# Where two groups of values and one projection of keys stand among the jobs of a graph attention kernel

## The chip, the cores and the metric

The kernel runs on one core of one Trainium2 chip. The metric is the device time in microseconds (us) of one execution. The input is fixed: 32 graphs of 256 nodes with 384 features, in float32.

## The reference, cut to what matters

For every graph, 12 heads of 32 features attend over 256 nodes, restricted to the edges of an adjacency matrix. The input is added back, and each row is normalised:

```python
q = split(x @ Wq + bq);  k = split(x @ Wk + bk);  v = split(x @ Wv + bv)   # 32 x 12 x 256 x 32
scores = q @ k.T / sqrt(32) + beta * adj
scores = where(adj > 0, scores, -9e15)
out = softmax(scores) @ v                       # per head, 256 x 32
x = layernorm(x + merge(out))                   # 32 x 256 x 384
```

## The kernel before, in words

All five engines run one long unrolled program, and semaphores join them. The 12 heads of a graph form three groups of four. TensorE computes the scores of a group at once (`scores`, line 463): 16 matmuls, each on a quarter of the array's rows (the profile writes 32*128), into four PSUM banks `s_bank`, one for each head of the group. VectorE then takes the maxima of a head from its bank (line 600), and ScalarE the exponentials (line 518). The exponentials of ten heads of a graph are turned by VectorE in blocks of 32 (line 635) and moved by DMAs into `shuffled`; those of heads 10 and 11 are turned by TensorE.

Everything else that TensorE does is a job, named by a letter, a part and a graph:

- X: a third of the input of a graph is transposed (line 396, two matmuls). ScalarE copies the high half out of PSUM (line 538) and VectorE then subtracts it to get the low half (line 616).
- K, Q: one group of keys or queries (line 387, nine matmuls of 256 columns), copied out by ScalarE (line 534).
- V: half of the nodes' values (line 384, nine matmuls of 384 columns), copied out by ScalarE (line 536).
- T: the exponentials of one head are turned (line 433, four matmuls), copied out by ScalarE (line 530).
- O: probabilities times values for one group of heads (`values`, line 416, 16 matmuls, each on a quarter of the array's columns, written 128*32), copied out by ScalarE (line 544).
- G: the result of an O job is turned back (`turn_heads`, line 424, two matmuls) and scaled by VectorE (line 623).

While the kernel works at the softmax of graph n, its jobs make the input of graph n + 2, the queries, keys and values of graph n + 1, and the output of graph n - 2. The function `jobs_of(n, h)` says by hand which jobs stand at head h. TensorE runs the jobs of head 0, then the second group's scores; those of heads 1 to 4, then the third group's scores; those of heads 5 to 8, then the first scores of graph n + 1; and then those of heads 9 to 11.

All jobs share four PSUM banks, `j_bank`, in rotation. The list `ring` is every job in program order, and the job at place r writes bank r modulo 4. Before its first instruction TensorE waits in `run` until the job at place r - 4 has been copied out, by ScalarE and VectorE both (`wait_taken`). ScalarE does the exponentials of head h + 2 and then takes the jobs of head h. VectorE has its own fixed order around head 9: the maxima of the next graph's head 0, the low half of the X job of head 9, the maxima of the next graph's head 1.

Of the kernel before, what the change touches and what calls it, by code (L numbers as in the profile page):

```python
# [34 lines left out]
def graph_attention_program(nc, x, adj, wq, bq, wk, bk, wv, bv, beta, out):  # L35
# [22 lines left out]
    def by_blocks(n, h):  # L58
        return h < block_heads(n)
# [5 lines left out]
    def jobs_of(n, h):  # L65
        if n == 0:

            jobs = {
                0: (("K", 2, 0),),
                1: (("K", 0, 1),),  # L70
                2: (("Q", 0, 1),),
                3: (("K", 1, 1),),
                4: (("V", 0, 0),),
                5: (("Q", 1, 1),),
                6: (("V", 1, 0), ("Q", 2, 1)),
                7: (("V", 0, 1),),
                9: (("X", 0, 2), ("K", 2, 1)),
                10: (("X", 1, 2),),
                11: (("X", 2, 2), ("V", 1, 1)),
            }  # L80
        elif n < B - 1:
            jobs = {
                0: (("O", 0, n - 2),),
                1: (("X", 0, n + 2), ("K", 0, n + 1)),
                2: (("G", 0, n - 2), ("Q", 0, n + 1)),
                3: (("K", 1, n + 1),),
                4: (("O", 1, n - 2),),
                5: (("X", 1, n + 2), ("Q", 1, n + 1)),
                6: (("G", 1, n - 2), ("Q", 2, n + 1)),
                7: (("V", 0, n + 1),),  # L90
                8: (("O", 2, n - 2),),
                9: (("X", 2, n + 2), ("K", 2, n + 1)),
                10: (("G", 2, n - 2),),
                11: (("V", 1, n + 1),),
            }
        else:
            jobs = {
                0: (("O", 0, n - 2),),
                1: (("O", 1, n - 2),),
                2: (("G", 0, n - 2), ("O", 2, n - 2)),  # L100
                3: (("G", 1, n - 2),),
                4: (("G", 2, n - 2),),
                5: (("O", 0, n),),
                7: (("G", 0, n), ("O", 0, n - 1)),
                8: (("O", 1, n - 1),),
                9: (("G", 0, n - 1), ("O", 2, n - 1), ("G", 1, n - 1), ("O", 1, n)),
                10: (("G", 2, n - 1), ("G", 1, n)),
            }
        turn = () if by_blocks(n, h) else (("T", h, n),)
        return turn + tuple(job for job in jobs.get(h, ()) if 0 <= job[2] < B)  # L110
# [4 lines left out]
    second_jobs = (("K", 1, 0),) + tuple(("X", c, 1) for c in range(C))  # L115
    last_jobs = (("O", 2, B - 1), ("G", 2, B - 1))
    ring = [*first_jobs, *second_jobs, *(job for n in range(B) for h in range(H) for job in jobs_of(n, h)), *last_jobs]
    place = {job: r for r, job in enumerate(ring)}

# [33 lines left out]
    with ctx:  # L153
# [216 lines left out]
        def _(pe):  # L370
# [124 lines left out]
            for n in range(B):  # L495
                for h in range(H):
                    jobs = jobs_of(n, h)
                    if not by_blocks(n, h):
                        run(jobs[0])
                        jobs = jobs[1:]  # L500
                    for job in jobs:
                        run(job)
                    if h % J == 0:
                        if h < H - J:
                            scores(n, h // J + 1)
                        elif n + 1 < B:
                            scores(n + 1, 0)
# [4 lines left out]
        def _(act):  # L512
# [58 lines left out]
            for n in range(B):  # L571
                for h in range(H):
                    s = H * n + h
                    if s + 2 < B * H:
                        exps(s + 2)
                    for job in jobs_of(n, h):
                        take(job)
# [388 lines left out]
```

## Time and profile before

| quantity | us |
|---|---|
| median of three runs | 622.64 (622.37 to 623.55) |
| the profiled execution's own time | 621.97 |
| its span | 620.1 |
| TensorE (PE) busy | 601.8, 97% |
| VectorE (DVE) busy | 582.7, 94% |
| ScalarE (ACT) busy | 574.8, 93% |
| GpSimd (POOL) busy | 492.6, 79% |

The profile comes from one execution. "PE" are TensorE's matmuls, "PEld" its weight loads, which run beside them. The ends of matmuls are modelled and the next one starts before the end of the last, so that for TensorE the starts are what can be compared. The granted clock of TensorE is shown as 1.00 (of 2.4 GHz) from 60 to 550 us.

### The profile page before, as it was taken

The page shows a single profiled execution, that of the slowest core. Times are in us where ns is not written, and L with a number is a line of the kernel's source. Part 1 is how long each engine was busy: PE and PEld are TensorE (multiplying, and loading weights), DVE is VectorE, ACT ScalarE, POOL GpSimd, SP SyncE. Part 2 cuts the span into 40 slices and gives each one's busy share as a digit, 9 for nine tenths or more (in the row PEclk, how much of TensorE's full clock was granted, in tenths as well). Part 3 has the DMA queues.
Part 4 walks back from the last instruction along what each step waited for, and adds up shares of the span by engine and source line. Part 5 has one row for each costly group of instructions (what it writes and reads, how often), then busy time and mean ns, then how long its engine had stood idle before and what let it go on. Part 6 is the DMA issues. An engine that isn't in the chain of part 4 may idle for free. (4 is left out here: it accounts for less than half of the span.)

```text
span 620.1 us, 20691 instructions
## 1 busy us (share of the span) xinstructions
PE 601.8 (97%) x6080; PEld 488.2 (79%) x6080; DVE 582.7 (94%) x2235; ACT 574.8 (93%) x2063; POOL 492.6 (79%) x669
## 2 busy tenths in 40 slices
PE   8999999999999999999999999999999999999991
PEld 7887878787888878787878788888878787878760
DVE  4989999999999999999999999999999999999786
ACT  4999999999999999999999999999999999999981
POOL 1334448988888888888898888898888889889793
PEclk9999999999999999999999999999999999999996
DMA  6258879988888988888998888898888898887832
GB/s 202 80 120 193 180 169 220 203 193 203 200 201 198 236 177 202 201 203 195 220 199 196 203 201 199 202 222 185 203 202 200 197 227 187 201 201 176 198 92 101
DMA packets 56190, 117.61 MB, mean 190 GB/s; under 512 B 10512, under 2 KB 12304, under 8 KB 56080
## 3 DMA queue, kind: packets, MB, share of 16 engines
q1 hardware_dynamic: 54992, 116.10, 80.6%
q8 instruction: 50, 0.82, 0.6%
q14 instruction: 60, 0.49, 0.3%
q10 hardware_dynamic: 1088, 0.20, 0.2%
HBM read 22.94 MB, written 12.58 MB: 57 GB/s over the span
## 5 line engine op out<-in xcount | busy, mean ns | idle before, releaser
L518 ACT ACTIVATE probs<-neg_scores,neg_max 128x256 f32<-128x256 f32 x768 | 382.5, 504 | 1.8 <-DVE neg_max L600 1.3
L600 DVE CUSTOM_DVE_ANT_0 neg_scores<-s_bank,bias_sb 128x256 f32<-128x256 f32 x768 | 280.1, 414 | 16.3 <-PE s_bank L463 15.1
L635 DVE STREAM_TRANSPOSE blocks<-probs 128x512 f32<-128x512 f32 x308 | 196.8, 685 | 0.3 <-ACT probs L518 0.3
L518 ACT ACTIVATION_READ_ACCUMULATOR probs<-neg_scores,neg_max 128x1 f32 x768 | 150.9, 197 | 0.0
L463 PE MATMUL s_bank<-qk 32*128 32x256 f32 x1536 | 110.0, 400 | 1.0 <-ACT qk L534 0.6
L387 PE MATMUL j_bank<-xt_high,w_high 128*128 128x256 f32 x567 | 110.1, 302 | 0.3 <-ACT qk L534 0.3
L534 ACT ACTIVATE qk<-j_bank,qk_bias 128x256 f32<-128x256 f32 x192 | 89.9, 469 | 21.0 <-PE j_bank L387 17.6
L463 PEld LDWEIGHTS s_bank<-qk 32*128 32x128 f32 x1536 | 69.5, 184 | 41.0 <-ACT qk L534 13.1
L898 POOL TENSOR_SCALAR att<-att,rstd,shift 128x384 f32<-128x384 f32 x58 | 95.7, 1656 | 6.3 <-POOL shift L895 6.3
L416 PE MATMUL j_bank<-shuffled,v_sb 128*32 128x256 f32 x1232 | 98.1, 385 | 0.2 <-ACT blocks L530 0.2
L387 PE MATMUL j_bank<-xt_high,w_low 128*128 128x256 f32 x567 | 97.0, 279 | 0.0
L387 PE MATMUL j_bank<-xt_low,w_high 128*128 128x256 f32 x567 | 96.9, 279 | 0.0
L862 POOL TENSOR_TENSOR att<-att,x_sb 128x768 f32<-128x768 f32 x30 | 55.5, 1850 | 39.2 <-DVE att L623 38.4
L387 PEld LDWEIGHTS j_bank<-xt_high,w_high 128*128 128x128 f32 x567 | 79.4, 189 | 2.3 <-issue 1.8
L387 PEld LDWEIGHTS j_bank<-xt_low,w_high 128*128 128x128 f32 x567 | 79.7, 188 | 0.0
L387 PEld LDWEIGHTS j_bank<-xt_high,w_low 128*128 128x128 f32 x567 | 79.6, 188 | 0.0
L843 POOL TENSOR_SCALAR bias_sb<-adj_sb 128x512 f32<-128x512 f32 x30 | 59.9, 1998 | 22.4 <-DMA adj_sb<-in_adj_dram 16.7
L846 POOL TENSOR_SCALAR adj_sb<-adj_sb,beta_col 128x512 f32<-128x512 f32 x31 | 62.1, 2004 | 13.3 <-DVE bias_sb L648 10.2
L856 POOL TENSOR_TENSOR x_sb<-x_sb,bv_row 128x768 f32<-128x768 f32 x32 | 59.1, 1848 | 8.2 <-DMA bv_row<-in_L_gnn_bv_dram 7.9
L416 PEld LDWEIGHTS j_bank<-shuffled,v_sb 128*32 128x32 f32 x1232 | 37.2, 109 | 35.2 <-issue 15.1
L600 DVE DVE_READ_ACCUMULATOR2_ANT neg_max<- 128x1 f32 x768 | 63.9, 83 | 0.0
L888 POOL TENSOR_SCALAR nt_b<-var_eps,rstd 128x1 f32<-128x1 f32 x174 | 58.3, 347 | 6.5 <-POOL rstd L881 6.2
(81 smaller groups left out, 918.4 us busy)
## 6 DMA issues: line engine op xcount, KB each, us to landing
shuffled<-blocks SPq DMA_DIRECT2D x480, 160.0 KB, 4.2
x_sb<-in_x_dram SPq DMA_DIRECT2D x32, 384.0 KB, 6.1
out_dram<-att SPq DMA_DIRECT2D x30, 384.0 KB, 4.0
adj_sb<-in_adj_dram SPq DMA_DIRECT2D x32, 256.0 KB, 6.2
shuffled<-blocks SPq DMA_DIRECT2D x16, 128.0 KB, 2.5
blocks<-in_L_gnn_Wq_dram SPq DMA_DIRECT2D x1, 576.0 KB, 5.7
blocks<-in_L_gnn_Wk_dram SPq DMA_DIRECT2D x1, 576.0 KB, 8.0
blocks<-in_L_gnn_Wv_dram SPq DMA_DIRECT2D x1, 576.0 KB, 5.0
```

What stands on the lines that cost most here:

```text
L387: mm = pe.matmul(b[:, 0:N], wp[:, q, c, a * P:(a + 1) * P], xp[:, n % 2, c, :], start=(m == 0), stop=(m == 3 * C - 1))
L416: mm = pe.matmul(b[HD * j:HD * (j + 1), 0:N], v_sb[:, n % 4, k, h * HD:(h + 1) * HD], probs_k, start=(k == 0), stop=(k == T - 1))
L463: mm = pe.matmul(s_bank[j][:, t * N:(t + 1) * N], qk[rows, n % 2, 0, g, t * P:(t + 1) * P], qk[rows, n % 2, 1, g, :], start=True, stop=True)
L518: nc.scalar.activation(probs[:, (T * s + t) % (T * NX), :], neg_scores[:, (T * s + t) % (T * NH), :], ACT.Exp, bias=neg_max[:, n % 2, t, h ...
L534: ins = nc.scalar.activation(qk[:, n % 2, q, a, :], b[:, 0:N], ACT.Identity, bias=qk_bias[:, q, a:a + 1])
L600: nc.vector.tensor_tensor_reduce(neg_scores[:, (T * s + t) % (T * NH), :], s_bank[h % J][:, t * N:(t + 1) * N], bias_sb[:, n % 2, t, :], - ...
L635: nc.vector.transpose(blocks[:, n % 2, :, h, :, :].rearrange("p k t q -> p t k q"), probs[:, slot:slot + T, :].rearrange("p t (k q) -> p t ...
L843: nc.gpsimd.tensor_scalar(key_order(bias_sb[:, n % 2, :, :]), by_keys(adj_sb[:, :, :]), 0.0, MASKED, ALU.is_le, ALU.mult).then_inc(not_edg ...
L846: nc.gpsimd.tensor_scalar(adj_sb[:, :, :], adj_sb[:, :, :], 0.0, beta_col[:, 0:1], ALU.max, ALU.mult).then_inc(adj_beta_ready, 1)
L856: nc.gpsimd.tensor_tensor(x_sb[:, n % XB, :, :], x_sb[:, n % XB, :, :], bv_row[:, :].unsqueeze(1).to_broadcast([P, T, D]), ALU.add).then_i ...
L888: b_at[t] = link(nc.gpsimd.tensor_scalar(nt_b[:, t:t + 1], var_eps[:, t:t + 1], rstd[:, t:t + 1], rstd[:, t:t + 1], ALU.mult, ALU.mult))
L898: nc.gpsimd.tensor_scalar(att[:, n % 3, t, :], att[:, n % 3, t, :], rstd[:, t:t + 1], shift[:, t:t + 1], ALU.mult, ALU.subtract).then_inc( ...
```

## The change

Only the table in `jobs_of` for the graphs in the middle (1 to 30) changes. The O job of the second group moves from head 4 to head 0, directly behind the O job of the first group. The K job of the third group moves from head 9 to head 4, where the O job stood.

```diff
         elif n < B - 1:
             jobs = {
-                0: (("O", 0, n - 2),),
+                0: (("O", 0, n - 2), ("O", 1, n - 2)),
                 1: (("X", 0, n + 2), ("K", 0, n + 1)),
...
-                4: (("O", 1, n - 2),),
+                4: (("K", 2, n + 1),),
...
-                9: (("X", 2, n + 2), ("K", 2, n + 1)),
+                9: (("X", 2, n + 2),),
```

No instruction is added or taken away. Since the bank of a job follows from its place in the ring, the banks turn with it. These are TensorE's rows of before from the X job of head 9 to the second scores (their first row only) in the middle of the program; the number behind `j_bank` is the bank:

```order
L396 MATMUL j_bank1<-ident,x_sb 128x128 x2
L387 MATMUL j_bank2<-xt_high,w_high 128x256 x3
L387 MATMUL j_bank2<-xt_low,w_high 128x256 x3
L387 MATMUL j_bank2<-xt_high,w_low 128x256 x3
L433 MATMUL j_bank3<-ident,probs 128x128 x4
L424 MATMUL j_bank0<-ident,heads_t 128x128 x2
L433 MATMUL j_bank1<-ident,probs 128x128 x4
L384 MATMUL j_bank2<-w_high,xt_high 128x384 x3
L384 MATMUL j_bank2<-w_high,xt_low 128x384 x3
L384 MATMUL j_bank2<-w_low,xt_high 128x384 x3
L416 MATMUL j_bank3<-shuffled,v_sb 32x256 x8
L463 MATMUL s_bank0<-qk 128x256
```

And the same place in the changed kernel:

```order
L396 MATMUL j_bank2<-ident,x_sb 128x128 x2
L433 MATMUL j_bank3<-ident,probs 128x128 x4
L424 MATMUL j_bank0<-ident,heads_t 128x128 x2
L433 MATMUL j_bank1<-ident,probs 128x128 x4
L384 MATMUL j_bank2<-w_high,xt_high 128x384 x3
L384 MATMUL j_bank2<-w_high,xt_low 128x384 x3
L384 MATMUL j_bank2<-w_low,xt_high 128x384 x3
L416 MATMUL j_bank3<-shuffled,v_sb 32x256 x8
L416 MATMUL j_bank0<-shuffled,v_sb 32x256 x8
L463 MATMUL s_bank0<-qk 128x256
```

The K job has gone from behind the X job, and the second O job has come. V (line 384) wrote the bank that K had used, and now writes the bank that X has used (2 in both rows); the second T (line 433) wrote X's bank before.

The other place on TensorE is ahead of the third scores, before:

```order
L387 MATMUL j_bank0<-xt_high,w_high 128x256 x3
L387 MATMUL j_bank0<-xt_low,w_high 128x256 x3
L387 MATMUL j_bank0<-xt_high,w_low 128x256 x3
L416 MATMUL j_bank1<-shuffled,v_sb 32x256 x8
L463 MATMUL s_bank0<-qk 128x256
```

and now:

```order
L387 MATMUL j_bank1<-xt_high,w_high 128x256 x3
L387 MATMUL j_bank1<-xt_low,w_high 128x256 x3
L387 MATMUL j_bank1<-xt_high,w_low 128x256 x3
L387 MATMUL j_bank2<-xt_high,w_high 128x256 x3
L387 MATMUL j_bank2<-xt_low,w_high 128x256 x3
L387 MATMUL j_bank2<-xt_high,w_low 128x256 x3
L463 MATMUL s_bank0<-qk 128x256
```

The O job between the second group's keys and the third scores has become the third group's keys.

## Rows read from the trace of the kernel before

**Rows 1.** Window: stretch, length, busy time (and count) by engine, clock, DMA.

```profile
311.47:329.82 18.35, 18.35 (x193) 14.91 (x189) 17.87 (x70) 17.64 (x65) 16.32 (x23) 1.00 0.88 203
```

**Rows 2.** Waits from 60 to 550 us: waiter, releaser, total, times, longest (us).

```profile
DVE neg_scores L600 <- PE s_bank L463: 10.2, 27, 1.0
```

**Rows 3.** Timeline, PE, first scores to second: start, duration, instruction.

```profile
305.30 1.15 PE L463 MATMUL s_bank<-qk 32*128 32x256 f32 x16
306.37 0.44 PE L396 MATMUL j_bank<-ident,x_sb 128*128 128x128 f32 x2
...
307.72 0.60 PE L433 MATMUL j_bank<-ident,probs 128*128 128x128 f32 x4
308.15 0.38 PE L424 MATMUL j_bank<-ident,heads_t 128*128 128x128 f32 x2
308.37 0.60 PE L433 MATMUL j_bank<-ident,probs 128*128 128x128 f32 x4
308.73 0.77 PE L384 MATMUL j_bank<-w_high,xt_high 128*128 128x384 f32 x3
...
310.47 1.07 PE L416 MATMUL j_bank<-shuffled,v_sb 128*32 128x256 f32 x16
...
311.47 1.15 PE L463 MATMUL s_bank<-qk 32*128 32x256 f32 x16
```

**Rows 4.** Timeline, PE, second group's keys, second O job, third scores.

```profile
315.17 0.52 PE L387 MATMUL j_bank<-xt_high,w_high 128*128 128x256 f32 x3
...
315.88 0.52 PE L387 MATMUL j_bank<-xt_high,w_low 128*128 128x256 f32 x3
316.32 1.07 PE L416 MATMUL j_bank<-shuffled,v_sb 128*32 128x256 f32 x16
317.32 1.15 PE L463 MATMUL s_bank<-qk 32*128 32x256 f32 x16
```

**Rows 5.** Timeline, PE, second and fourth round of an O job.

```profile
322.88 0.39 PE L416 MATMUL j_bank<-shuffled,v_sb 128*32 128x256 f32 x2
...
323.31 0.39 PE L416 MATMUL j_bank<-shuffled,v_sb 128*32 128x256 f32 x2
```

**Rows 6.** Timeline, graphs 0 and 1: scores straight behind a K job, a maximum.

```profile
18.24 0.51 PE L387 MATMUL j_bank<-xt_high,w_low 128*128 128x256 f32 x3
18.68 1.15 PE L463 MATMUL s_bank<-qk 32*128 32x256 f32 x16
...
42.08 0.51 PE L387 MATMUL j_bank<-xt_high,w_low 128*128 128x256 f32 x3
...
42.47 0.08 DVE L600 DVE_READ_ACCUMULATOR2_ANT neg_max<- 128x1 f32 x1
...
42.70 1.15 PE L463 MATMUL s_bank<-qk 32*128 32x256 f32 x16
```

**Rows 7.** Timeline, DVE: maxima, low half of X, G job; last, maxima behind third scores.

```profile
306.64 0.42 DVE L600 CUSTOM_DVE_ANT_0 neg_scores<-s_bank,bias_sb 128x256 f32<-128x256 f32 x1 [0.37 <-PE s_bank L463]
...
307.43 0.42 DVE L616 TENSOR_TENSOR xt_low<-j_bank,xt_high 128x256 fp32r<-128x256 f32 x1
...
308.57 0.42 DVE L623 TENSOR_TENSOR att<-j_bank,inv_sum 128x256 f32<-128x256 f32 x1
...
318.74 0.38 DVE L600 CUSTOM_DVE_ANT_0 neg_scores<-s_bank,bias_sb 128x256 f32<-128x256 f32 x1
```

**Rows 8.** Timeline, ACT: end of head 11's exponentials, then the high half of X.

```profile
306.93 0.19 ACT L518 ACTIVATION_READ_ACCUMULATOR probs<-neg_scores,neg_max 128x1 f32 x1
...
307.02 0.37 ACT L538 ACTIVATE xt_high<-j_bank 128x256 fp32r<-128x256 f32 x1
```

**Rows 9.** Timeline in graph 0: a T job held by the low half of X.

```profile
34.29 0.42 DVE L616 TENSOR_TENSOR xt_low<-j_bank,xt_high 128x256 fp32r<-128x256 f32 x1 [0.74 <-ACT xt_high L538]
...
34.78 0.42 PEld L433 LDWEIGHTS j_bank<-ident,probs 128*128 128x128 f32 x4 [0.36 <-ACT qk L534]
```

## The prediction

> **What bounds the kernel now.** I read the page's shares first: PE 97%, DVE 94%, ACT 93% leave no engine much room. I then took one graph in the middle as a window [rows 1]. It lasts 18.35 us, and the matmul row is busy for all of it; VectorE works 17.87 us, ScalarE 17.64. The table of waits shows VectorE waiting for scores once per graph: 10.2 us in 27 times is 0.38 each [rows 2]. It is the wait for the first scores of the next graph [rows 7], and on no other scores does VectorE wait, so TensorE's order sets the period, and VectorE could follow a graph down to about 18.35 - 0.38 = 17.97. What counts is when TensorE starts each job.
>
> I count from the start of the first scores, 305.30 [rows 3]. X starts at 1.07, T at 2.42 (K lies between), V at 3.43, O at 5.17, the second scores at 6.17. From there to the third scores it is 317.32 - 311.47 = 5.85 [rows 3, 4]. The rest of a graph, 6.33 from third scores to first, is untouched.
>
> **Stretch 1, first scores to second: K leaves, O comes.** Without a wait, TensorE would go X, T, G, T, V. A pair of transposes ahead of a T takes 0.22 (308.15 to 308.37), T to G 0.43 (307.72 to 308.15), the second T to V 0.36 [rows 3]. V could start at 1.07 + 0.22 + 0.43 + 0.22 + 0.36 = 2.30, that is 1.13 earlier than now.
>
> But V's bank is now X's. Of X's copies the late one is the low half on VectorE: it starts at 307.43 and takes 0.42, so it ends at 307.85, which is 2.55 [rows 7]. It can't come earlier. On VectorE it stands behind the two maxima of head 0, which wait for the first scores [rows 7]; these are pinned to our zero. On ScalarE the high half it needs runs from 307.02 to 307.39 [rows 8], behind work fed by the part of the graph that doesn't change. Before, the job that used X's bank was the second T, at 3.07: it had half a microsecond to spare. In graph 0 a T job was held by just such a low half: that ended at 34.29 + 0.42 = 34.71 and the weights of T began to load at 34.78, 0.07 later [rows 9]. (The releaser printed there is another, since the wait is for two engines; the low half ended last.) So V starts at 2.55 + 0.07 = 2.62 and not at 2.30: the wait costs 0.32 us in each graph. Nothing covers it: TensorE works in order, and O and the second scores are queued behind.
>
> The other new neighbours don't bind. The first T wants the bank of the third group's queries, copied long before. The second T needs the exponentials of head 11, which end at 306.93 + 0.19 = 307.12, at 1.82 [rows 8]; it wants to start at 1.94, and even 0.1 late it is hidden by V's wait. The second O wants G's bank, which VectorE frees at 308.57 + 0.42, at 3.69 [rows 7]; O comes after 4.
>
> V to O stays 310.47 - 308.73 = 1.74. O behind O is not in the trace. An O job is four rounds; two last 323.31 - 322.88 = 0.43 [rows 5], so four back to back give 0.86, the lower end. The upper end is O as it stands now, with the change of array shape on both sides: 1.00 to the scores [rows 4] and 0.08 ahead of it (K's last triple to O takes 0.44, K's own step is (315.88 - 315.17)/2 = 0.36), 1.08. I take 0.90: the shape stays, which puts it near the lower end, with a little for the new weights. Then the last O to the second scores, 1.00. Sum: 2.62 + 1.74 + 0.90 + 1.00 = 6.26 against 6.17: **+0.09**.
>
> **Stretch 2, second scores to third: O leaves, K comes.** From the start of the second group's keys to the third scores it is now 317.32 - 315.17 = 2.15 [rows 4]. After: one K job at 3 x 0.355 = 1.06, the new one's first to last triple 0.71, and last triple to scores. That last step is in the trace twice: 0.44 in graph 0 (18.24 to 18.68) and 0.62 in graph 1 (42.08 to 42.70) [rows 6]. In the second, the last of the maxima that those scores must wait for ended only at 42.47 + 0.08 = 42.55 [rows 6], so that one holds a wait and I take 0.44; the lower end is K's own 0.36, the upper 0.62. Sum 2.21: **+0.06**. The new K's bank (the first group's keys) and the banks of those after it are freed as before or earlier.
>
> ScalarE gets an O copy (0.37) ahead of head 3's exponentials and loses a K copy (0.47) behind X; its sum stays, and it has 0.71 us idle per graph [rows 1]. VectorE's list doesn't change. The maxima that each set of scores must wait for are earlier relative to it, since both stretches grow. The third scores come 0.15 later after the first ones; VectorE now takes them at 318.74, 1.42 after their start, where it can at 1.34 [rows 4, 7], so it may wait 0.07 there, out of its 0.38. DMA and GpSimd work is the same and follows.
>
> **Sum.** +0.15 us per graph. V's wait exists where a graph has both an X job at head 9 and a G job of an earlier graph: graphs 2 to 29, 28 times. 28 x 0.15 = 4.2 us. In graphs 1 and 30 K moves without the wait, worth under 0.1 each way; I leave them at nothing. The profiled execution took 621.97 (span 620.1 and 1.9 around it) and would take 626.2. The median shown is 0.67 above it, so I predict 622.64 + 4.2 = **626.8 us**, slower by 0.7%.
>
> A rule weighed: the Trainium skill says (TensorEngine Tiling (Array Packing), Key Properties) that changing the tiling mode drains TensorE. The change has one such switch fewer per graph, eight against nine. The trace agrees that a switch costs something: 0.44 against 0.36 from K into O, and 1.00 against 0.86 from O's first round to the scores [rows 4, 5]. By the rule alone the kernel gets faster; the size is the first rival's, which stands on rows.
>
> **Rivals.**
> 1. *No wait for V's bank, only the saved switches: faster.* V at 2.30 gives stretch 1 = 5.94, -0.23; with stretch 2, -0.17 per graph, -4.8 us: 617.9. VectorE's floor of 17.97 per graph would let it through. For it: each of the steps is a row. Against: the low half's end at 2.55 is fixed by two engines. It decides if the low half ends before 2.25. Chance 0.18, with what lies between it and no change.
> 2. *It comes out even.* The wait is there, but O behind O costs 0.86 and K into scores 0.36: +0.15 - 0.04 - 0.08 = +0.03 per graph, 0.8 us, 623.5. Chance 0.10.
> 3. *Switches are not saved at all.* O behind O 1.08, K into scores 0.62: 0.15 + 0.18 + 0.18 = +0.51, 14.3 us, 636.9. Against: the 0.62 holds a wait. Chance 0.07, mostly for a part of it.
> 4. *ScalarE falls behind:* its second O copy pushes X's high half, and with it VectorE's low half and the maxima of heads 6 and 7, by up to 0.37. VectorE's 0.38 of idle time takes that up; only beyond it does it show. With both fully on the path +0.37 x 28 = 10 us more, 637. Chance 0.03.
>
> **Numbers.** Forecast 0.62, its own range 624.0 to 630.5 (O behind O at 0.86 to 1.00, K into scores 0.36 to 0.50, the wait 0.05 either way). A difference of 0.2%, 1.25 us, is about what a measurement of this kernel can tell from none. Slower 0.62 + 0.07 + 0.03 = 0.72, same 0.10, faster 0.18. For 8 in 10 the range is 618.5 to 630.5: below it some 0.08, above it 0.1.
>
> **What would show it.** In a graph of the changed profile: the weight load of V (line 384) behind the second T idle for about 0.3 us, released by VectorE's low half (line 616) or put down to ScalarE; V's first matmul 2.6 us after the first scores; O to O about 0.9; K's last triple to the third scores 0.44; the period 18.50. The first rival is right if V starts at 2.3 and the period is 18.2. The third shows as O to O above 1.0. VectorE's wait at the first scores should stay at 0.4 to 0.5, with a second small one at the third scores. Were the granted clock to leave 1.00 in the middle, all of it would be off.

## The result: slower by 0.9%

| quantity | before | after |
|---|---|---|
| median of four runs, us | 622.50 (622.25 to 623.55) | 627.78 (626.88 to 629.17) |
| ratio of the runs, 95% interval | 1 | 1.0089 (1.0076 to 1.0101) |
| span of the profiled execution, us | 620.1 | 627.3 |

The forecast was 626.8 (range 618.5 to 630.5), 4.2 us above before; measured are 5.3 at the medians. In a second measurement of the same kernel, five rounds on one chip with the experiments below, it took 627.44 against 622.81, ratio 1.0072 (1.0058 to 1.0086).

The profile of the changed kernel, its first part (busy time, share of the span, instructions):

```profile
span 627.3 us, 20691 instructions
PE 606.3 (97%) x6080; PEld 493.1 (79%) x6080; DVE 585.6 (93%) x2235; ACT 575.2 (92%) x2063; POOL 491.3 (78%) x669
```

The counts are those of before; every engine does the same work, TensorE in more time. The span grew by 7.2 us, more than the medians, and part of that isn't the change. Windows of the changed kernel's profile show it: two graphs, and the start (columns: stretch, length, busy time and count of PE, PEld, DVE, ACT, POOL, granted clock, DMA share, GB/s):

```profile
317.34:335.89 18.55, 18.51 (x192) 15.09 (x188) 18.01 (x70) 17.64 (x66) 16.26 (x23) 1.00 0.87 201
335.89:354.40 18.51, 18.46 (x193) 15.04 (x189) 17.97 (x70) 17.64 (x66) 16.25 (x23) 1.00 0.87 200
10.00:20.00 10.00, 7.94 (x49) 6.46 (x47) 6.83 (x20) 5.68 (x14) 1.71 (x1) 0.68 0.48 172
```

The first of the two graphs, whose rows are shown below, takes 18.55 us against 18.35 [rows 1], but it is one of the slower ones. Over the graphs from 60 to 550 us the median is 18.51 and the mean 18.52; before they are 18.35 and 18.36. So a graph costs 0.16 us more, and 28 times 0.16 is 4.5 us, close to the 4.6 between the medians of the second measurement. The span's other 2.7 us lie mostly in the start: from 10 to 20 us the granted clock averages 0.68, a part of the stretch at the lower of its two levels, where this window of the profile of before shows 1.00. Just ahead TensorE had waited 1.2 us for the low half of a weight. In the second profile of the same kernel the granted clock was 1.00 in that window, the second set of scores came at 18.83 us (18.68 before), and the span was 624.9, so I leave the start out.

Now the stretch that the prediction timed, in the timeline of TensorE (start, duration, instruction), from the first scores to the second and on to the third:

```profile
311.09 1.15 PE L463 MATMUL s_bank<-qk 32*128 32x256 f32 x16
312.17 0.44 PE L396 MATMUL j_bank<-ident,x_sb 128*128 128x128 f32 x2
312.44 0.60 PE L433 MATMUL j_bank<-ident,probs 128*128 128x128 f32 x4
312.88 0.38 PE L424 MATMUL j_bank<-ident,heads_t 128*128 128x128 f32 x2
313.10 0.60 PE L433 MATMUL j_bank<-ident,probs 128*128 128x128 f32 x4
313.74 0.76 PE L384 MATMUL j_bank<-w_high,xt_high 128*128 128x384 f32 x3
...
315.48 1.93 PE L416 MATMUL j_bank<-shuffled,v_sb 128*32 128x256 f32 x32
317.34 1.15 PE L463 MATMUL s_bank<-qk 32*128 32x256 f32 x16
...
322.10 0.52 PE L387 MATMUL j_bank<-xt_high,w_high 128*128 128x256 f32 x3
...
322.81 0.52 PE L387 MATMUL j_bank<-xt_high,w_low 128*128 128x256 f32 x3
323.25 1.15 PE L463 MATMUL s_bank<-qk 32*128 32x256 f32 x16
```

V starts 313.74 - 311.09 = 2.65 after the first scores. From the second T to V it takes 0.64, where it took 0.36 [rows 3]: V waits 0.28 us. The two O jobs run as one row of 32 matmuls, and reach the scores in 1.86 instead of twice 1.00. Both stretches come out at 6.25 and 5.91.

The waiting weight load on PEld, and the instruction on VectorE before it:

```profile
313.71 0.47 PEld L384 LDWEIGHTS j_bank<-w_high,xt_high 128*128 128x128 f32 x3 [0.25 <-issue]
```

```profile
313.22 0.42 DVE L616 TENSOR_TENSOR xt_low<-j_bank,xt_high 128x256 fp32r<-128x256 f32 x1
```

The low half of X ends at 313.22 + 0.42 = 313.64, and V's weights load 0.07 later, the same 0.07 as in [rows 9]. It is 0.07 in each of the 26 waits of V's weights between 60 and 550 us. But the profile writes "issue" and names no releaser. In the table of waits from 60 to 550 us, which the page orders by total, it looks as harmless:

```profile
DVE neg_scores L600 <- PE s_bank L463: 12.6, 27, 1.2
PEld j_bank L384 <- issue: 6.6, 26, 0.3
```

6.6 us in 26 times is 0.25 per graph, more than the 0.16 that the whole change loses, in a row that names nobody. A reader who trusts the name would look for it elsewhere; experiments 1, 2 and 4 decide. VectorE's own wait stays at the first scores, 0.47 each now.

### The profile page after: what moved, and what is told of

The parts are those of the page before. It is cut to its first block and busy times, and to the rows that moved or that the text cites. A ratio compares the mean times of both kernels' runs of the same rounds, so it can differ in the third digit from the quotient of the medians.

```text
span 627.3 us, 20691 instructions
## 1 busy us (share of the span) xinstructions
PE 606.3 (97%) x6080; PEld 493.1 (79%) x6080; DVE 585.6 (93%) x2235; ACT 575.2 (92%) x2063; POOL 491.3 (78%) x669
## 5 line engine op out<-in xcount | busy, mean ns | idle before, releaser
L387 PE MATMUL j_bank<-xt_high,w_high 128*128 128x256 f32 x567 | 108.5, 299 | 0.3 <-ACT w_high L550 0.3
L416 PE MATMUL j_bank<-shuffled,v_sb 128*32 128x256 f32 x1232 | 92.1, 383 | 0.2 <-ACT blocks L530 0.2
L416 PEld LDWEIGHTS j_bank<-shuffled,v_sb 128*32 128x32 f32 x1232 | 40.2, 109 | 36.3 <-issue 15.1
```

The source lines that it names most:

```text
L387: mm = pe.matmul(b[:, 0:N], wp[:, q, c, a * P:(a + 1) * P], xp[:, n % 2, c, :], start=(m == 0), stop=(m == 3 * C - 1))
L416: mm = pe.matmul(b[HD * j:HD * (j + 1), 0:N], v_sb[:, n % 4, k, h * HD:(h + 1) * HD], probs_k, start=(k == 0), stop=(k == T - 1))
```

## Experiments

The ratios are to the kernel before, measured on the same chip beside each experiment. All line numbers are those of the kernel that ran; where its table is a line shorter, line 463 is 462, and so on.

**1. The wait taken away.** V goes ahead of the second T. X's bank then falls to T, and V's is that of the third O job.

```diff
-                10: (("G", 2, n - 2),),
-                11: (("V", 1, n + 1),),
+                10: (("G", 2, n - 2), ("V", 1, n + 1)),
```

> The changed kernel with V ahead of the second T (jobs of head 10: T, G, V; of head 11: T), so that X's bank goes to T, which comes 1.7 us later, and V takes the bank of the third O job, long free. Theory (V's wait for the low half of X costs 0.28 us per graph, the rest of the change saves): V starts 1.9 us after the first scores, the stretch to the second scores shrinks from 6.26 to about 5.95, a graph takes 18.25 us, the kernel about 619 us, faster than before. Rival (the stretch is long for another reason, and the wait is only where the slack shows): the time stays at 627.

Measured: 618.05 us against 622.81, ratio 0.9921 (0.9907 to 0.9936): faster than both. TensorE's timeline:

```profile
305.35 1.15 PE L462 MATMUL s_bank<-qk 32*128 32x256 f32 x16
306.43 0.44 PE L395 MATMUL j_bank<-ident,x_sb 128*128 128x128 f32 x2
306.70 0.60 PE L432 MATMUL j_bank<-ident,probs 128*128 128x128 f32 x4
307.14 0.38 PE L423 MATMUL j_bank<-ident,heads_t 128*128 128x128 f32 x2
307.27 0.76 PE L383 MATMUL j_bank<-w_high,xt_high 128*128 128x384 f32 x3
...
308.92 0.60 PE L432 MATMUL j_bank<-ident,probs 128*128 128x128 f32 x4
309.45 1.93 PE L415 MATMUL j_bank<-shuffled,v_sb 128*32 128x256 f32 x32
311.31 0.50 PE L462 MATMUL s_bank<-qk 32*128 32x256 f32 x4
```

V starts 1.92 after the first scores and the second ones 5.96 after them, 0.29 less than in the changed kernel; its table of waits has no row for V's weights any more. The same jobs with two neighbours exchanged turn a loss of 0.7% (1.0072 in this measurement) into a gain of 0.8%. The rival falls.

**2. The wait alone, in the kernel before.** Only K moves, from behind X to behind V. O stays, no change of array shape is saved, and V takes X's bank.

```diff
-                9: (("X", 2, n + 2), ("K", 2, n + 1)),
+                9: (("X", 2, n + 2),),
...
-                11: (("V", 1, n + 1),),
+                11: (("V", 1, n + 1), ("K", 2, n + 1)),
```

> The kernel before with nothing moved but the K job of the third group, from behind X to behind V, still ahead of the second scores. O stays where it was, no change of array shape is saved, and the work between two sets of scores is that of before; but V now takes X's bank. Theory: the wait alone costs 0.28 us per graph, the stretch from first to second scores takes 6.46 instead of 6.18, the kernel 622.5 + 28 x 0.28 = 630.3 us. Rival (the wait is absorbed by slack elsewhere): 622 to 623.

Measured: 631.12 us, ratio 1.0133 (1.0117 to 1.0149).

```profile
310.26 1.15 PE L463 MATMUL s_bank<-qk 32*128 32x256 f32 x16
...
312.91 0.76 PE L384 MATMUL j_bank<-w_high,xt_high 128*128 128x384 f32 x3
...
315.70 1.07 PE L416 MATMUL j_bank<-shuffled,v_sb 128*32 128x256 f32 x16
316.71 1.15 PE L463 MATMUL s_bank<-qk 32*128 32x256 f32 x16
```

V is again 2.65 behind the first scores, and the second scores come at 6.45 instead of 6.17. The wait costs its full length. It also prices the saved switch: the changed kernel has the same wait and took 627.44 in the same measurement, 3.7 us less, 0.13 us per graph. The rows agree: the first of two O jobs takes 1.86 - 1.00 = 0.86 instead of 1.00, and K steps into the scores in 0.44 (322.81 to 323.25 above), as it stepped into O. The difference of the two times also holds what the pace of some projections does (last section), which is a few hundredths of a microsecond per graph.

**3. The O job alone.** K stays behind X.

```diff
-                0: (("O", 0, n - 2),),
+                0: (("O", 0, n - 2), ("O", 1, n - 2)),
...
-                4: (("O", 1, n - 2),),
```

> Only the O job of the second group is moved to head 0; K stays behind X, so V does not take X's bank. One change of array shape fewer and no wait. Theory: on TensorE alone a graph would take 18.31 (621 us). But the second scores come 7.05 after the first ones; VectorE then waits about 0.7 us for them and has only 0.38 to give, so it becomes the engine that sets the period: about 18.7 us per graph, 632 us, with VectorE waiting at the second scores and not at the first, and TensorE waiting for VectorE ahead of the third or first scores. Rival (the saved switch decides): 621 us.

Measured: 636.35 us, ratio 1.0221 (1.0201 to 1.0242), 4 us more than I had expected. The scores on TensorE, in a whole graph from second to second:

```profile
301.31 1.15 PE L462 MATMUL s_bank<-qk 32*128 32x256 f32 x16
...
305.72 0.52 PE L386 MATMUL j_bank<-xt_high,w_low 128*128 128x256 f32 x3
306.31 1.15 PE L462 MATMUL s_bank<-qk 32*128 32x256 f32 x16
...
309.65 0.51 PE L386 MATMUL j_bank<-xt_high,w_low 128*128 128x256 f32 x3
310.36 0.77 PE L383 MATMUL j_bank<-w_high,xt_high 128*128 128x384 f32 x3 [0.20 <-issue]
...
313.13 1.15 PE L462 MATMUL s_bank<-qk 32*128 32x256 f32 x16
...
320.15 1.15 PE L462 MATMUL s_bank<-qk 32*128 32x256 f32 x16
```

VectorE in the same graph:

```profile
306.08 0.09 DVE L599 DVE_READ_ACCUMULATOR2_ANT neg_max<- 128x1 f32 x1
...
309.83 0.43 DVE L615 TENSOR_TENSOR xt_low<-j_bank,xt_high 128x256 fp32r<-128x256 f32 x1
...
321.50 0.42 DVE L599 CUSTOM_DVE_ANT_0 neg_scores<-s_bank,bias_sb 128x256 f32<-128x256 f32 x1 [0.65 <-ACT probs L517]
```

A graph takes 18.84. The second scores come 7.02 behind the first, VectorE waits 0.65 for them (1.35 behind 320.15; the releaser printed is again another), and then it has no slack left. The delay comes back to TensorE in two places. The expected one is small: ahead of the third scores K's last triple takes 0.59 instead of 0.44, since the last maximum ends only at 306.17, 0.14 ahead of them (0.15 in [rows 6]). The larger is once more a bank of an X job: V's first matmul of the next stretch stands at 310.36, 0.10 behind the low half's end at 310.26, and 0.71 behind the triple before it (309.65), where without a wait it takes 0.35. Together that is 0.51 us, the difference between the 18.84 measured and the 18.31 to 18.35 of TensorE alone. I had the engine right and the size short, since I had counted VectorE's list and not the jobs that wait for its copies. The K job has to move with O to keep the stretches even; alone, the saved switch is worth nothing.

**4. The low half later, in both kernels.** The only change is on VectorE: at head 9 the second head's maxima come ahead of X's low half.

```diff
-                        if h != 2 * J + 1 and s + 4 < B * H:
+                        if s + 4 < B * H:
                             maxima(s + 4)
                         for job in jobs_of(n, h):
                             take(job)
-                        if h == 2 * J + 1 and s + 4 < B * H:
-                            maxima(s + 4)
```

In the changed kernel:

> The changed kernel with one thing moved on VectorE: at head 9 the low half of X comes behind the maxima of two heads of the next graph and not of one. Theory (V waits for exactly this instruction): the low half ends at about 3.15 after the first scores and not at 2.55, V starts at about 3.25, 0.6 us per graph more, 28 x 0.6 = 17 us, 644 us. Rival (V waits for something else, such as ScalarE's copy or the exponentials of head 11): 627 us or a little less.

In the kernel before:

> The same move on VectorE in the kernel before. There X's bank belongs to the second T, whose weights load at 2.96 after the first scores. Theory: of the 0.6 us by which the low half is later, 0.45 fall into T's slack, and T waits 0.2 to 0.26 us: 28 times, 6 to 7 us, 629 us. Rival (the wait costs as much here as in the changed kernel, since all is one loop): 639 us; or nothing: 622.5 us.

Measured: 644.40 us, ratio 1.0354 (1.0340 to 1.0368), and 629.50 us, ratio 1.0112 (1.0098 to 1.0126). In the changed kernel, TensorE (the first scores stand at 317.21) and VectorE:

```profile
320.46 0.76 PE L384 MATMUL j_bank<-w_high,xt_high 128*128 128x384 f32 x3 [0.65 <-issue]
```

```profile
319.93 0.42 DVE L616 TENSOR_TENSOR xt_low<-j_bank,xt_high 128x256 fp32r<-128x256 f32 x1
```

In the kernel before, the second T's weights and VectorE:

```profile
312.36 0.42 PEld L433 LDWEIGHTS j_bank<-ident,probs 128*128 128x128 f32 x4 [0.22 <-ACT qk L534]
```

```profile
311.87 0.42 DVE L616 TENSOR_TENSOR xt_low<-j_bank,xt_high 128x256 fp32r<-128x256 f32 x1
```

The low half ends at 320.35 and V starts 0.11 later, 3.25 behind the first scores where it was 2.65; it ends at 312.29 and T's weights load 0.07 later. One instruction put back by 0.6 us costs 17 us in one kernel and 7 in the other (28 x 0.60 and 28 x 0.25; the 627.44 of the changed kernel was measured on another chip), and the difference is the slack that X's bank had before the change. That slack was 0.34 us: the weights of the second T loaded 2.96 behind the first scores, and could have at 2.55 + 0.07 = 2.62. The expectation had put it at 0.45. This shows the releaser that the profile doesn't name.

**5. A step of the reckoning that was wrong.** After transposes the first three matmuls of a K or Q job take 0.43 instead of 0.35. If that is a price, transposes should stand together. I moved the second G job from behind a Q job to straight behind X: in the kernel of experiment 1, there also together with the first G job, and in the kernel before.

```diff
-                5: (("X", 1, n + 2), ("Q", 1, n + 1)),
-                6: (("G", 1, n - 2), ("Q", 2, n + 1)),
+                5: (("X", 1, n + 2), ("G", 1, n - 2), ("Q", 1, n + 1)),
+                6: (("Q", 2, n + 1),),
```

> V ahead of the second T as in the version that ran 618 us, and the second G job moved from behind the Q job of its stretch to straight behind the X job, so that the transposes there stand together and the two Q jobs too. No bank wait should come of it. Theory (TensorE's starts set the period, and each step from transposes into a projection costs 0.09 us on top, the first triple taking 0.43 instead of 0.35): 0.09 us less in the stretch ahead of the first scores, 28 times 2.5 us, 615.6 us. Rival (VectorE already sets the period with V's wait gone): 618 us.

> The same with the first G job moved as well, straight behind the X job of the stretch ahead of the third scores. Theory: another 0.09 us per graph, 613 us; VectorE's floor of 17.98 us per graph is then just reached (18.23 - 0.18 = 18.05). Its danger is new: G needs ScalarE's copy of the first O job, which ends 1.0 us after the second scores start, and wants it at 1.27. Rival (that copy or VectorE comes late): no gain over the version with the second G job alone, or a loss.

> The kernel before with only the second G job moved straight behind the X job of its stretch; nothing of the studied change. Theory: 0.09 us less per graph, 620.1 us. Rival (the order of transposes and projections costs nothing): 622.6 us.

Measured: 617.74 us, ratio 0.9933 (0.9920 to 0.9945), no different from experiment 1; with both G jobs 618.86, ratio 0.9953 (0.9940 to 0.9967), no gain and 1.1 us more than with one; in the kernel before 623.26, ratio 1.0019 (1.0010 to 1.0028), slightly slower. That last kernel's timeline:

```profile
301.23 0.44 PE L396 MATMUL j_bank<-ident,x_sb 128*128 128x128 f32 x2
301.50 0.39 PE L424 MATMUL j_bank<-ident,heads_t 128*128 128x128 f32 x2
301.65 0.59 PE L387 MATMUL j_bank<-xt_high,w_high 128*128 128x256 f32 x3
```

X to G takes 0.27, where in the kernel before X (306.37 in [rows 3]) to K takes 0.20:

```profile
306.57 0.60 PE L387 MATMUL j_bank<-xt_high,w_high 128*128 128x256 f32 x3
```

The projection's long first triple only gives back what its early first matmul had taken, and the order costs nothing. The theory falls, and so does VectorE as the reason: in the first of the three it still waits for scores 8.9 us in 27 times, 0.33 each:

```profile
DVE neg_scores L599 <- PE s_bank L462: 8.9, 27, 0.9
```

**The changed kernel again,** beside experiments 1 to 3:

> The changed kernel again, beside the others on one chip. Both theories: 627 to 628 us; its start should be that of before, and a graph 18.55 us.

It took 627.44 us, span 624.9. Over the 27 graphs in the middle of its profile the three stretches have the medians 6.26, 5.87 and 6.38, and the whole graph 18.51. The 18.55 expected is the length of one of the slower graphs. In the profile of before the medians are 6.17, 5.85 and 6.32.

## Why the prediction was right

The mechanism was right: +0.16 us per graph against +0.15, and V's wait for X's bank is the cause. How close the sum came is in part luck, since two small misses in it have opposite signs.

- *V waits for X's bank, from 2.30 to 2.62.* Right, and shown by experiments 1, 2 and 4. V starts at 2.65: its weights load at 2.62, as worked out, and its first matmul stands 0.03 behind them, a step that the forecast left out. The wait is 0.28 and not 0.32, because X to T takes 0.27 and not the 0.22 read from another pair of transposes; V would have gone at 2.37.
- *The second T had half a microsecond to spare.* It had 0.34 (experiment 4): its weights load before its first matmul, and they are what waits. The sum doesn't use this number.
- *V to O 1.74, O to O 0.90, O to scores 1.00.* The first is 1.74, the other two together 1.86, so that O behind O is 0.86, the low end. Stretch 1 was put at 6.26 and is 6.25 to 6.26; V's 0.03 and this 0.04 cancel.
- *K's last triple to the third scores 0.44; stretch 2 +0.06.* The step is 0.44, and from the new K job's first matmul to the scores it takes 1.15, 0.71 + 0.44. The stretch is 5.91 in the graph shown, as worked out, but 5.87 in the median, +0.02, since one of its projections runs quicker in most graphs (last section).
- *ScalarE, VectorE and the other banks don't bind.* Right. VectorE's wait at the first scores is 0.47, within the 0.4 to 0.5 of the forecast; the small second one at the third scores, which the forecast thought possible, doesn't show.
- *The third stretch is untouched, 6.33.* This is the term that was mis-sized: it takes 6.38, +0.06 at the medians. Its order, and its waits, are those of before, but some projections in it run at another pace (last section). This miss and that of stretch 2, both of pace and neither foreseen, nearly cancel: 18.50 was forecast and 18.51 is the median.
- *The rule on tiling modes.* The Trainium skill (TensorEngine Tiling (Array Packing), Key Properties) says that a change of mode drains TensorE. One change fewer does help, by 0.13 us per graph (experiments 1 and 2). The bank's wait of 0.28 is larger.

## What to carry to other kernels

In a rotation of buffers, moving one job changes the buffer of every job behind it: after any move, list again who waits for whose buffer, with the time at which each is freed. Here the gain of a better order was there all the time, and exchanging V with the second T, so that the bank freed late goes to a job that wants it 1.7 us later, made the move pay (0.9921 instead of 1.0072, measured side by side). When engines are this evenly loaded, a move must also keep the distance between the points at which another engine is fed: half of this change, the O job alone, costs more than the whole (1.0221).

## What the runs showed of the hardware that I had not expected

The same nine matmuls run at two paces with the clock granted in full. The first Q job of the third stretch in the kernel before, and the same job in the changed one:

```profile
318.59 0.59 PE L387 MATMUL j_bank<-xt_high,w_high 128*128 128x256 f32 x3
319.02 0.50 PE L387 MATMUL j_bank<-xt_low,w_high 128*128 128x256 f32 x3
319.36 0.51 PE L387 MATMUL j_bank<-xt_high,w_low 128*128 128x256 f32 x3
319.70 0.38 PE L424 MATMUL j_bank<-ident,heads_t 128*128 128x128 f32 x2
```

```profile
324.53 0.60 PE L387 MATMUL j_bank<-xt_high,w_high 128*128 128x256 f32 x3
324.97 0.51 PE L387 MATMUL j_bank<-xt_low,w_high 128*128 128x256 f32 x3
325.32 0.52 PE L387 MATMUL j_bank<-xt_high,w_low 128*128 128x256 f32 x3
325.67 0.38 PE L424 MATMUL j_bank<-ident,heads_t 128*128 128x128 f32 x2
```

Three matmuls take 0.34 us in one and 0.35 in the other, 1.11 against 1.14 for the job. Which jobs are quick stays the same for many graphs and differs between the kernels. In the kernel before it changes once, near 409 us, with nothing changed in the program: the third stretch takes 6.32 us in every graph ahead of that and 6.38 to 6.39 in every one behind it, while the second goes from 5.85 to 5.81. Beside GpSimd's long operations, VectorE, ScalarE and the DMA traffic in three kernels, I found none that goes with the quick jobs in all three. The cause is open; no experiment was made for it. It moves a stretch by 0.03 to 0.06 us here. The last kernel of experiment 5 takes 18.38 us per graph in the mean, against 18.36 before; that is 0.6 of the 1.2 us by which it is slower, and where the rest comes from is not shown.
